# The order of VectorE's attention-score masks and router levels in a fused attention and expert-FFN kernel

## What is computed

```python
x = x + _L0_xattn_ref(ctx_1024, _layernorm(x), mask, ...)   # keys: 256 tokens and 77 context rows, 4 heads of 64
#   sim = qn @ kn.T ; masked keys = -max ; softmax ; @ v ; @ W_out + b_out
x = x + _L0_ffn_ref(_layernorm(x), gate, bias, up, down, shared_up, shared_down)
#   scores = sigmoid(x @ gate.T); best of 2 groups of 4 experts; top 2 of 8; weights normalised, * 2.5
#   out = sum_e w_e * relu(x @ up_e.T)**2 @ down_e.T + relu(x @ shared_up.T)**2 @ shared_down.T
```

## Time and profile before

| | |
|---|---|
| median of 3 runs | 1337.84 us (1335.99 to 1338.17) |
| the profiled execution | 1337.32 us, its span 1335.5 us |
| mean granted clock of TensorE | 0.988 of full speed |
| PE busy | 1243.6 us, 93% of the span |
| PE weight loads busy | 1102.9 us, 83% |
| DVE busy | 1036.1 us, 78% |
| ACT busy | 759.3 us, 57% |
| POOL busy | 536.4 us, 40% |

### The profile page before, as it was taken

The page is one execution under the profiler, slowest core; times in us unless marked ns, Lnnn a source line. Parts: engine busy times, 40 slices in busy tenths (PEclk is TensorE's granted clock), DMA queues, the critical chain, the costliest instruction groups (busy, mean ns, idle before and its releaser), DMA issues.

```text
span 1335.5 us, 29598 instructions
## 1 busy us (share of the span) xinstructions
PE 1243.6 (93%) x10176; PEld 1102.9 (83%) x10176; DVE 1036.1 (78%) x3561; ACT 759.3 (57%) x1733; POOL 536.4 (40%) x477
## 2 busy tenths in 40 slices
PE   3799999999999999999999999999999999999997
PEld 2588888888888888888888888888888888888886
DVE  3678877778877778877778877778877778877775
ACT  3566555656555656555656555656555656555652
POOL 4234444334444334444334444334444334444332
PEclk9799999999999999999999999999999999999998
DMA  4000000000000000000000000000000000000000
GB/s 141 11 12 20 20 20 19 2 20 20 20 20 19 1 20 20 20 20 20 2 20 20 20 20 19 2 20 20 20 20 20 2 20 20 20 20 19 2 9 17
DMA packets 28228, 25.86 MB, mean 19 GB/s; under 512 B 6640, under 2 KB 27536, under 8 KB 28080
## 3 DMA queue, kind: packets, MB, share of 16 engines
q1 hardware_dynamic: 27744, 23.83, 5.7%
q0 software_dynamic: 336, 0.14, 0.2%
HBM read 15.57 MB, written 8.39 MB: 18 GB/s over the span
## 4 chain that ended last, share of the span: by engine, by line
PE 40%; issue 25%; DVE 13%; ACT 12%; POOL 9%; DMA 1%; DVEq 0%; ACTq 0%; POOLq 0%
PE up_ps L261 6%; PE attn_ps L356 6%; PE up_ps L263 6%; PE up_ps L262 6%; ACT probs L618 5%; PE attn_ps L370 4%; POOL k_scale L1134 4%; ACT relu L663 3%; ACT relu_sb L658 3%; DVE masked L831 3%; POOL ln_lo L1145 3%; DVE acc L997 2%; PE attn_ps L309 2%; PE down_ps L261 2%; PE down_ps L262 2%
## 5 line engine op out<-in xcount | busy, mean ns | idle before, releaser
L1177 POOL TENSOR_TENSOR hid_lo<-relu,hid_hi 128x512 fp32r<-128x512 f32 x192 | 246.9, 1286 | 442.2 <-DVE hid_hi L982 442.2
L261 PE MATMUL down_ps<-down_hi,hid_hi 128*128 128x256 f32 x768 | 234.3, 305 | 14.6 <-issue 12.5
L261 PE MATMUL up_ps<-x_hi,up_hi 128*128 128x256 f32 x768 | 230.0, 299 | 2.7 <-ACT x_hi L647 1.2
L997 DVE SCALAR_TENSOR_TENSOR acc<-down_ps,route_w,acc 128x256 f32<-128x256 f32 x512 | 221.4, 474 | 2.8 <-PE down_ps L263 2.4
L262 PE MATMUL up_ps<-x_lo,up_hi 128*128 128x256 f32 x768 | 216.3, 282 | 0.0
L263 PE MATMUL up_ps<-x_hi,up_lo 128*128 128x256 f32 x768 | 216.3, 282 | 0.0
L263 PE MATMUL down_ps<-down_hi,hid_lo 128*128 128x256 f32 x768 | 215.8, 281 | 0.0
L262 PE MATMUL down_ps<-down_lo,hid_hi 128*128 128x256 f32 x768 | 215.5, 281 | 0.0
L618 ACT ACTIVATE probs<-masked,neg_max,q_scale 128x333 f32<-128x333 f32 x256 | 167.6, 656 | 73.6 <-DVE neg_max L838 73.6
L982 DVE CAST hid_hi<-relu 128x512 fp32r<-128x512 f32 x192 | 124.5, 648 | 83.9 <-ACT relu L663 83.6
L658 ACT ACTIVATE relu_sb<-up_ps 128x512 f32<-128x512 f32 x192 | 114.6, 597 | 129.2 <-PE up_ps L263 123.2
(11 more groups left out here) (147 smaller groups left out, 2820.6 us busy)
## 6 DMA issues: line engine op xcount, KB each, us to landing
x_in<-in_x SPq DMA_DIRECT2D x32, 256.0 KB, 2.8
out<-acc SPq DMA_DIRECT2D x32, 256.0 KB, 2.1
c_in<-in_ctx SPq DMA_DIRECT2D x32, 77.0 KB
up_stage<-in_up_t SPq DMA_DIRECT2D x1, 1536.0 KB, 12.2
down_stage<-in_down_t SPq DMA_DIRECT2D x1, 1536.0 KB, 15.0
mask_in<-in_mask SPq DMA_DIRECT2D x32, 9.6 KB, 2.6
w_stage<-in_w_kv SPq DMA_DIRECT2D x1, 512.0 KB, 5.6
w_stage<-in_w_q SPq DMA_DIRECT2D x1, 256.0 KB, 5.0
```

Source lines behind the costliest of these rows:

```text
L261: nc.tensor.matmul(out_ap, s_hi, m_hi, start=first, stop=False)
L997: nc.vector.scalar_tensor_tensor(acc[:, t, :], down_ps[:, (e + 1) % 2, t * D:(t + 1) * D], route_w[:, t, e:e + 1], acc[:, t, :], ALU.mult, ...
L1177: nc.gpsimd.tensor_tensor(hid_lo[:, p % HID_RING, :], relu2[:, p % 2, :], hid_hi[:, p % HID_RING, :], ALU.subtract).then_inc(hid_lo_done, 1)
```

## The change

Only the written order of DVE's calls in `step` changes; no call is added or removed, and the lists of PE, ACT, POOL and SP stay the same.

```diff
                 mask_scores(b, 0, first)
                 mask_scores(b, 1, first)
-                routing(1, 2, 3, 4, 5, 6)
                 mask_scores(b, 2, first)
                 mask_scores(b, 3, first)
-                routing(7)
                 negate_max(b, 0)
-                routing(8)
                 high(2)
-                routing(9, 10)
+                routing(1, 2, 3, 4, 5, 6, 7)
                 mask_scores(b, 4, first)
                 mask_scores(b, 5, first)
-                routing(11, 12)
+                routing(8, 9, 10)
                 if experts:
                     add_shared(f, f_first)
-                routing(13)
                 mask_scores(b, 6, first)
                 mask_scores(b, 7, first)
-                routing(14)
                 negate_max(b, 1)
-                routing(15, 16)
+                routing(11, 12, 13, 14, 15, 16)
                 if following:
                     layer_norm1(b + 1, False)
```

## The result

The changed kernel takes 1341.68 us (median of 7 runs), the kernel before 1336.49 us in the same comparison. The ratio is 1.0032, with a 95% interval from 1.0020 to 1.0044: slower by 4.3 us, between 2.7 and 5.9. The profiled execution has a span of 1339.8 us, against 1335.5. One of the seven runs, at 1657.55 us and a mean granted clock of 0.674, is a slow one that the ratio and its interval leave out.

What follows compares the result with a forecast made beforehand. PE, busy 38.44 of 40.06 us a step, was taken to bound the kernel. 30 x 0.13 - 0.57 = +3.3 us took 1337.32 to 1340.6 profiled, so 1341.1 us median; range 1333 to 1346.

Steps and rivals of the forecast that it cites:

- The gap at transpose 0: PE's 0.57 us wait before transpose 0, thirty times, after the last score pair; claimed to go.
- the hold on `above`: DVE's `above` standing still under POOL's low part of couple 2; its removal claimed to gain 1.11 us.
- DVE's row: DVE from `sig_den`'s old place to the layer norm; gains and losses claimed to sum to 0.36 us later.
- the spacing of dependent levels: Router levels on DVE newly in a row, without other work between; claimed loss 0.76 us.
- The hold on `biased`: DVE's `biased` held for the whole rest of POOL's low part of couple 2; claimed loss 0.82 us.
- The faster rival: `biased` isn't held, DVE 0.46 us early, all 31 gaps of 0.57 us gone: 17.7 us faster, 1320; chance 0.15.
- the product: PE's `down_expert(f, 2)`, awaiting couple 3's low part; claimed to start 0.13 us later, with a new 0.70 us gap.
- Step 31: Step without a layer norm, where the 0.57 us was claimed to be won.
- The race behind the cast: POOL starts before `sig_den` behind couple 2's cast: 17.7 us slower, 1355.5; chance 0.06 together with `score` held.
- The even exchange: DVE only 0.25 instead of 0.36 us late, so the total change is 0: 1337.8; chance 0.33.
- The sum of expert 0: DVE's sum that frees the bank for `down_expert(f, 2)`; claimed to end near 646.74 and not be the last.

Runs made afterwards that it cites:

- the second half alone: Kernel before, with only levels 11 to 16 in one row behind the last mask and the second negated maxima: 1344.33 us, ratio 1.0048.
- the third: Changed kernel with POOL's `x_res` ahead of `q_scale` instead of behind it, without a wait: 1456.1 us, ratio 1.0907.

## Why the prediction was right, point by point

- **What bounds the kernel.** Right. The gap at transpose 0 belonged to the mask of unit 4 and to the hold on `above`, not to ACT, as the waits view has it. With `above` free, ACT no earlier and the rest of the order untouched, it goes.
- **DVE's row.** Said: 0.36 us late at the layer norm. Measured: 8.97 us from 636.36 to 645.33 where it was 8.58, so 0.39. By terms: the mask of unit 2 waits 0.24 us (0.23 said); `sig_den` to `score` 0.20 (0.20); cast to POOL 0.50 (0.50); `biased` to `pair_hi` 1.02 where it was 0.21, so 0.81 lost (0.82); `above` to `tied` 0.21 (0.20). The rest, the spacing of dependent levels, is then 0.78 where 0.76 was said, and the second half alone shows it as a cost of its own. One sum is slightly off: the cast of couple 2 comes out at 635.75 by its terms and not at 635.73, which changes nothing, as POOL and `sig_den` move with it.
- **The hold on `biased`,** the one price that no row had, was full: it ends 0.04 us behind POOL, though it is smaller than any held operation with two SBUF inputs in the trace before (`sig_den`, just as small, has one input and was held too). The rule of the Trainium skill, page "SBUF — State Buffer", section "Who interferes with whom", that two SBUF inputs are enough whatever the operation's length, agrees with 0.99 us for an operation of 0.17. The faster rival rested on its opposite.
- **On PE.** Said: 0.57 us goes, 0.70 comes, net 0.13. Measured from start to start: 0.65 goes and 0.76 comes. I took the first from the idle time in the row and not from the distance of the starts, which left both too small by nearly the same. Against the same point of PE's row the product starts 0.15 us later than before (649.06 less 1.90, against 647.01), where 0.13 was said. The steps became 0.157 us longer in the mean of 29 and 0.14 by the medians.
- **The other ends.** Step 31 gained 0.32 us where 0.57 was said (35.95 to 35.63 us from its `exp_neg` to the next). Up to the output projection it had gained 0.60 (24.07 to 23.47 us); then the transposes of `x_hat` (L410) took 0.69 us at a granted clock of 0.50, where they had taken 0.44 at full clock, and PE's row lost 0.29 us there. 29 x 0.157 - 0.32, 0.05 us more up to step 2 and nothing (0.01 less) behind step 31 make the 4.3 us between the spans; 3.3 were predicted. That the time itself, 1341.1 us, lies within 0.6 of the 1341.68 measured is in part luck: it started from a median 1.35 us higher than that of the comparison, and added 1 us less.
- **The rivals.** The race behind the cast was not lost: `sig_den` takes 0.17. The even exchange was near: what separates it is a tenth of a microsecond a step, and its bound, 0.2% from no change, is where the measured interval begins (1.0020). DVE's row tells them apart more clearly: 0.39 us late, where the even case ended at 0.34. The sum of expert 0, which I had noted as not the last, was only 0.3 us from being so (its rows end at 648.67, the low part at 648.96), and the early cast of couple 3 won nothing because the sum then came 0.26 us later itself. My estimate of 0 to 8 us had taken it as unmoved and was right only at its lower end.
- **What I hadn't seen** was in the experiments, not in the forecast: that `x_res` moved next to `x_hat` would hold it. A tensor-scalar operation within SBUF had been held in the trace before (`sig_den`, 0.51 us for 0.17), and I took POOL's recorded starts as if nothing ahead of them could be held. In the run `x_res` is recorded from 631.15, behind the 630.98 at which `x_hat` would have ended.

## What to carry to other kernels

Ask of each DVE operation that would run beside a POOL operation where its inputs are: here those with two SBUF inputs (`above`, 1.39 us for 0.29), and casts (1.05 for 0.42) and tensor-scalar operations (`sig_den`, 0.51 for 0.17) within SBUF, stood still until POOL's difference or sum had ended, and those that read PSUM (the masks, 0.50) or were reciprocals (0.17) did not. Place the operation that starts POOL so that readers of PSUM follow it. A removed gap is worth something only up to the next place where the same row of DVE is awaited, so follow the row to that place before counting. And independent work between the members of a dependent chain is not in the way of the chain: it is what pays for 0.12 us a link, and, ahead of an operation that waits for another engine, for that wait.

## What the runs showed of the hardware that was not expected

- A POOL operation held DVE ahead of its own recorded start. `x_res` is recorded from 631.15 to 632.41, yet the first tile of `x_hat`, recorded from 630.24, 0.91 us earlier, ended only behind it, after 2.32 us. With the same `k_scale` running but `x_res` held behind a semaphore, both tiles took their 0.41 us. So `k_scale` alone, though recorded over the same time, held nothing, and with `x_res` queued behind it there was a hold. That POOL's next operation takes hold while the one ahead still computes is an inference from these runs. The profile's spans on POOL are rough, so `x_res` may also have begun earlier than it is recorded; nothing here separates the two.
- With a gap of 2.0 us in PE's row in every step, a stretch at 1.2 GHz came behind each such gap in two kernels and behind 20 of 30 in the third, and in the one shown PE had no gap at all in that stretch. Gaps of 0.4 to 0.8 us a step (both kernels and all other experiments) left the mean granted clock of the profiled executions at 0.987 or more.
